# Image keys of ten batches by seven products for eight blocks

## What is computed

```
q = _heads(hidden_states @ to_q_w)                       # (16, 512, 640) @ (640, 640)
h_txt = _sdpa(q, _heads(ehs_txt @ to_k_w), _heads(ehs_txt @ to_v_w))
...
h_ip = _sdpa(q, _heads(ehs_ip @ to_k_ip_w), _heads(ehs_ip @ to_v_ip_w))   # (16, 427, 1024) @ (1024, 640)
out = _merge(h_txt) + _merge(h_obj) + _merge(h_oth) + _merge(h_ip)
out = out @ to_out_w + to_out_b + hidden_states
```

## Time and profile before

| what | us |
|---|---|
| median of 3 runs | 2381.95 (2381.77 to 2382.32) |
| the profiled execution | 2381.67 |
| its span, first to last instruction | 2379.5 |
| TensorE busy | 2365.9 (99%), 12801 matmuls |
| VectorE busy | 1835.2 (77%) |
| ScalarE busy | 1775.6 (75%) |
| GpSimd busy | 412.5 (17%) |

### The profile page before, as it was taken

How to read it: one execution, slowest core, us unless ns; L and a number is a source line. 1 busy time by engine, 2 the same in 40 slices (tenths; PEclk the granted TensorE clock), 3 DMA queues, 4 the chain that set the end, 5 groups by cost and what they waited for, 6 DMA issues and landing times.

```text
span 2379.5 us, 37663 instructions
## 1 busy us (share of the span) xinstructions
PE 2365.9 (99%) x12801; PEld 1805.1 (76%) x12801; DVE 1835.2 (77%) x3291; ACT 1775.6 (75%) x3906; POOL 412.5 (17%) x564
## 2 busy tenths in 40 slices
PE   9999999999999999999999999999999999999999
PEld 8999999998999986566666666666666666666665
DVE  4457777732333489999999999999999999999994
ACT  4343433332223369999999999999999999999995
POOL 0000000000000023413223133133132231231310
PEclk9999999999999999999999999999999999999999
DMA  9445444374644555545555555555455555555542
GB/s 339 161 128 159 150 136 141 109 268 147 232 167 174 182 174 153 148 129 154 152 143 146 134 148 159 137 146 151 128 156 154 134 150 141 144 161 128 147 132 78
DMA packets 371749, 370.12 MB, mean 156 GB/s; under 512 B 110046, under 2 KB 298590, under 8 KB 371558
## 3 DMA queue, kind: packets, MB, share of 16 engines
q1 hardware_dynamic: 334384, 306.14, 46.7%
q10 hardware_dynamic: 37174, 61.59, 7.0%
HBM read 215.57 MB, written 83.89 MB: 126 GB/s over the span
## 4 chain that ended last, share of the span: by engine, by line
PE 97%; ACT 2%; issue 0%; DMA 0%; DVE 0%; ACTq 0%
PE st_ps L1661 17%; PE s_ps L489 13%; PE st_ps L509 12%; PE om_ps L523 12%; PE om_ps L544 11%; PE om_ps L567 11%; PE s_ps L1713 7%; PE om_ps L1713 4%; PE s_ps L1681 3%; PE st_ps L1713 3%; ACT s_ps L689 1%; PE om_ps L1730 1%; ACT probs L681 1%; PE om_ps L602 1%; PE st_ps L1621 0%
## 5 line engine op out<-in xcount | busy, mean ns | idle before, releaser
L689 ACT ACTIVATE s_ps<-s_ps,negmax 128x427 f32<-128x427 f32 x1280 | 767.8, 608 | 21.6 <-DVE small L759 21.6
L750 DVE TENSOR_REDUCE negmax<-s_ps 128x2 f32<-128x854 f32 x640 | 666.0, 1041 | 75.4 <-PE s_ps L489 69.1
L681 ACT ACTIVATE probs<-st_ps 128x1024 f32<-128x1024 f32 x632 | 656.1, 1038 | 15.2 <-PE st_ps L509 3.7
L489 PE MATMUL s_ps<-kpack,qpack 96*128 96x512 f32 x1280 | 420.9, 410 | 2.1 <-ACT s_ps L689 2.1
L509 PE MATMUL st_ps<-qpack,kpack 104*128 104x512 f32 x1264 | 405.4, 402 | 2.5 <-ACT probs L681 2.5
L447 POOL TENSOR_TENSOR small<-small,negmax 128x616 f32<-128x616 f32 x160 | 196.5, 1228 | 999.8 <-DVE negmax L767 999.6
L1661 PE MATMUL st_ps<-ctx_split,w_split_ip 128*128 128x428 f32 x1848 | 364.2, 358 | 0.0
L1661 PEld LDWEIGHTS st_ps<-ctx_split,w_split_ip 128*128 128x128 f32 x1848 | 347.4, 188 | 15.2 <-issue 1.0
L489 PEld LDWEIGHTS s_ps<-kpack,qpack 96*128 96x128 f32 x1280 | 223.4, 189 | 177.6 <-ACT s_ps L689 81.0
L544 PE MATMUL om_ps<-xs,wq 128*128 128x512 f32 x1200 | 340.6, 394 | 0.0
L567 PE MATMUL om_ps<-heads,wo 128*128 128x512 f32 x1125 | 320.8, 394 | 0.0
(11 more groups left out here) (116 smaller groups left out, 2437.8 us busy)
## 6 DMA issues: line engine op xcount, KB each, us to landing
qpack<-q_out SPq DMA_DIRECT2D x240, 256.0 KB, 4.7
kpack<-kT SPq DMA_DIRECT2D x240, 217.5 KB, 2.9
kT<-k_out ACTq DMA_DIRECT2D x154, 217.5 KB, 3.3
ctx_split_raw<-in_ctxT SPq DMA_DIRECT2D x128, 214.0 KB, 4.6
tok_pair<-in_ctxT SPq DMA_DIRECT2D x48, 512.0 KB, 4.7
xs_raw<-in_xT SPq DMA_DIRECT2D x85, 256.0 KB, 3.8
out<-in_xT SPq DMA_DIRECT2D x75, 256.0 KB, 4.0
out_yT<-out SPq DMA_DIRECT2D x75, 256.0 KB, 2.1
```

The lines of the kernel that those rows point to most:

```text
L489: last = nc.tensor.matmul(s_ps[:, n % 2, z, :], qpack[r][0:ROWS_S, j, t * P:(t + 1) * P], kpack[r][0:ROWS_S, j, :], start=True, stop=True)
L681: nc.scalar.activation(probs[:, at:at + 2, :], transposed(u, duo), ACT.Exp).then_inc(p_done, 1)
L689: last = nc.scalar.activation(s_ps[:, n % 2, z, SMALL:TOK], s_ps[:, n % 2, z, SMALL:TOK], ACT.Exp, bias=negmax[:, r, IP, j, t:t + 1], accu ...
L750: nc.vector.tensor_reduce(negmax[:, r, IP, j, t0:t0 + 2], s_ps[:, n % 2, :, SMALL:TOK], AX_X, ALU.max, negate=True).then_inc(s_max, 1)
```

## The change

Batches 1 to 10 are taken in five pairs. The 640 key channels are 4 blocks of 128 and a fifth. For the four, weights are cut in 2 x 2 (512 context channels by 256 key channels) and a pair's context in 2 (halves of the context channels) x 2 (batches), and seven products take the place of eight. The fifth block is computed as before. A pair is 18 groups (`K_GROUPS`: operand, bank, tile) of 12 matmuls. Its eight operands are staged one after the other, as 4 x 428 columns, in three slots (`K_SLOTS`). GpSimd makes the sums T3, T2, T4 and T1 (`key_sum`), VectorE the sums of the weights once (`key_weight_sums`) and ten additions of PSUM banks per pair (`add_group`), two of which leave their sum in SBUF as u3.

Besides: the pairs' stores go to the sync queue (`store_group`), and so do raw loads of 876 KB each (`load_raw`); the small values' steps stand between the first four tiles of text values, and the quarters of the image-value weights are loaded only when the small values are stored; their sums (`weight_sums`) move from tile ("v", 3, 0) to ("v", 0, 0); `wq` and `x` are loaded at the start of batch 11 instead of batch 5.

```diff
+K_OPERANDS = (B11, T3, T2, T4, B21, T1, B22, "B12")
+K_SLOTS = 3
+K_GROUPS = ((0, "X", 0), (0, "X", 1), (0, "F", 0), (1, "Q", 0), (1, "Q", 1), (2, "U", 0), (2, "U", 1),
+            (3, "Q", 0), (3, "Q", 1), (4, "X", 0), (4, "X", 1), (4, "F", 0), (5, "U", 0), (5, "U", 1),
+            (6, "U", 0), (6, "U", 1), (6, "F", 1), (7, "F", 1))
+K_OUT = {7: (0, 2), 8: (0, 3), 9: (0, 0), 10: (0, 1), 11: (0, 4), 12: (1, 2), 13: (1, 3), 14: (1, 0), 15: (1, 1), 17: (1, 4)}
...
     for run in V_TXT:
-        ORDER += [("v", run, t) for t in range(len(tiles(run)))]
+        for t in range(len(tiles(run))):
+            ORDER.append(("v", run, t))
+            if run == V_TXT[0]:
+                ORDER.append(("s", 2 + t, 0))
...
     for run in range(TXT, RUNS):
-        ORDER += [("k", run, m) for m in k_slots(run)]
-        ORDER += {TXT + 1: [("s", 2, 0)], TXT + 2: [("s", 3, 0)]}.get(run, [])
+        if run - TXT not in K_PAIRED:
+            ORDER += [("k", run, m) for m in k_slots(run)]
+        elif K_PAIRED.index(run - TXT) % 2 == 0:
+            ORDER += [("p", K_PAIRED.index(run - TXT) // 2, i) for i in range(len(K_GROUPS))]
...
-    SUMS[("v", 3, 0)] = ("a", 0)
+    SUMS[("v", 0, 0)] = ("a", 0)
...
+    SUMS[("k", before_pairs, 4)] = ("sw", 0)
+    for i, part in ((0, S3), (1, S2), (4, S1), (5, S4)):
+        SPLITS[("p", 0, i)] = [("sw", part, 0)]
+    for pp in range(len(K_PAIRS)):
+        ahead = [("k", before_pairs, 3), ("p", 0, 0)] if pp == 0 else [("p", pp - 1, 15), ("p", pp - 1, 17)]
+        for j, step in enumerate(ahead + [("p", pp, i) for i in (2, 3, 6, 9, 11, 13)]):
+            SPLITS.setdefault(step, []).append(("z", pp, j))
+    T_SUMS = {}
+    for pp in range(len(K_PAIRS)):
+        ahead = [("k", before_pairs, 4), ("p", 0, 0)] if pp == 0 else [("p", pp - 1, 16), ("p", pp, 0)]
+        for i, step in zip((T3, T2, T4, T1), ahead + [("p", pp, 3), ("p", pp, 7)]):
+            T_SUMS[step] = (i, pp)
...
+        def store_group(pp, i):
+            run, m = pair_block(pp, i)
+            k0 = k_num(run, m)
+            sp.wait_ge(k_lo, k0 + 1)
+            sp.wait_ge(k_fill, k0 - k_base(TXT) + 1)
+            for part in (HI, LO):
+                sp.dma_start(d["kT"][run - TXT, part, m * P:(m + 1) * P, N_TXT:TOK],
+                             k_out[:, k0 % KR, part, 0:SM + IPN - 1].bitcast(F32)).then_inc(k_stored[k0 % KR], 16)
...
+        sp.wait_ge(s_acc, 4)
+        sp.wait_ge(sv_stored, 32)
         load_quarter(w_ops_raw[:, LO, A11, :, :], 0, 0)
...
+            elif kind == "z":
...
+                nc.scalar.activation(slots[z % K_SLOTS][:, HI, :, :], z_raw(which, n), ACT.Copy).then_inc(piece_hi, 1)
...
+            elif kind == "z":
...
+                hi, lo, raw = slots[r][:, HI, :, :], slots[r][:, LO, :, :], z_raw(which, n)
...
+        def add_group(pp, i):
...
+            if i in (5, 6):
...
+                nc.vector.tensor_tensor(u2, bank(pp, "U", t), u2, ALU.add).then_inc(u_add, 1)
+                dve.wait_ge(u_add, n + 2 * t + 1)
+                nc.vector.tensor_tensor(u3, bank(pp, "Q", t), u2, ALU.add).then_inc(u_add, 1)
+            elif i in (7, 8, 14, 15):
...
+                nc.vector.tensor_tensor(bank(pp, kind, t), bank(pp, kind, t), u2, ALU.add).then_inc(u_add, 1)
+            elif i in (12, 13):
...
+                nc.vector.tensor_tensor(u3, bank(pp, kind, t), u3, ALU.add).then_inc(u_add, 1)
...
+            if kind == "p":
+                add_group(a, b)
+                if b - 1 in K_OUT:
+                    keep_group(a, b - 1)
+                if b == len(K_GROUPS) - 1:
+                    keep_group(a, b)
...
+        def key_sum(i, pp):
...
+            if i == T3:
...
+                to, a, b, op = t3_raw[:, :, :], b22, b12, ALU.subtract
+            elif i == T2:
...
+                to, a, b, op = t2_raw[:, :, :], t3_raw[:, :, :], b11, ALU.add
+            elif i == T4:
+                stage_done(pool, z_number(pp, 3) - K_SLOTS)
...
+                to, a, b, op = z_raw(pp, 3), b21, t2_raw[:, :, :], ALU.subtract
+            else:
+                stage_done(pool, z_number(pp, 5) - K_SLOTS)
+                to, a, b, op = z_raw(pp, 5), b12, b11, ALU.subtract
+            nc.gpsimd.tensor_tensor(to, a, b, op).then_inc(t_raw, 1)
...
+        def k_group(pp, i):
...
+            if i == 0 or K_GROUPS[i - 1][0] != j:
+                pe.wait_ge(piece_lo, split_upto(("z", pp, j)))
+                if j in (1, 2, 5, 6):
+                    pe.wait_ge(piece_lo, split_upto(("sw", {1: S3, 2: S2, 5: S1, 6: S4}[j], 0)))
...
+            elif i in (7, 8):
+                pe.wait_ge(u_add, U_ADDS * pp + 2 * (t + 1))
```

More of the change, by code:

```diff
@@ L58 @@
 OP_PARTS = ((B11, B22), (B22, T4), (T4, OPS))
+K_PAIRS = ((1, 2), (3, 4), (5, 6), (7, 8), (9, 10))
+K_PAIRED = tuple(b for pair in K_PAIRS for b in pair)
+K_OPERANDS = (B11, T3, T2, T4, B21, T1, B22, "B12")
[4 more added lines that the diff above has]
+K_OUT = {7: (0, 2), 8: (0, 3), 9: (0, 0), 10: (0, 1), 11: (0, 4), 12: (1, 2), 13: (1, 3), 14: (1, 0), 15: (1, 1), 17: (1, 4)}
+K_OUT_ORDER = tuple(K_OUT.values())
+U_ADDS = 10
+S_PARTS = (S1, S2, S3, S4)
 V_TILES = 3
@@ L964, in project_context @@
     assert in_pair1 + pair_size + size(2, 2, CH) <= in_w_ops
+    s_w, s_w_raw = both("s_weights", [P, len(S_PARTS), 2, CC2, 2 * P], in_top)
+    raw = [at(f"ctx_raw{r}", [P, 2, 2, CC2, IPN], F32, at0) for r, at0 in enumerate((in_c0, in_c1))]
+    in_slots = in_top + size(len(S_PARTS), 2, CC2, 2 * P)
+    slot_size = size(2, CC2, IPN)
+    slots, slots_raw = zip(*(both(f"k_ops{r}", [P, 2, CC2, IPN], in_slots + r * slot_size) for r in range(K_SLOTS)))
+    in_sums = in_slots + K_SLOTS * slot_size
+    t3_raw = at("t3_raw", [P, CC2, IPN], F32, in_sums)
+    t2_raw = at("t2_raw", [P, CC2, IPN], F32, in_sums + size(CC2, IPN))
+    u2_k = at("u2_k", [P, 2, IPN], F32, in_sums + 2 * size(CC2, IPN))
+    u3_k = at("u3_k", [P, 2, IPN], F32, in_sums + 2 * size(CC2, IPN) + size(2, IPN))
+    assert in_sums + 2 * size(CC2, IPN) + 2 * size(2, IPN) <= end
     w, w_raw = {"k_txt": w0, "v_txt": w2}, {"k_txt": w0_raw, "v_txt": w2_raw}
@@ L988, in project_context @@
     sv_stored = sem("sv_stored")
+    sq_in, s_sum = sem("sq_in"), sem("s_sum")
+    raw_in = [[[sem(f"raw_in{r}_{h}{k}") for k in range(2)] for h in range(2)] for r in range(2)]
+    t_raw = sem("t_raw")
+    z_acc, u_acc, x_sb, u_add = sem("z_acc"), sem("u_acc"), sem("x_sb"), sem("u_add")
     d["late"] = LateKeys(w_ip, c0, k_late, k_stored, k_fill)
@@ L1006, in landed @@
     def landed(load):
-        return 16 * sum(buffer(n) == buffer(load) for n in range(load + 1))
+        return 16 * sum(buffer(n) == buffer(load) and LOAD_RUN[n] - TXT not in K_PAIRED for n in range(load + 1))
     def is_txt(run):
@@ L1043, in k_base, with k_num @@
         return run * QC
+    def k_num(run, m):
+        b = run - TXT
+        if b not in K_PAIRED:
+            return k_base(run) + m
+        first, second = K_PAIRS[K_PAIRED.index(b) // 2]
+        return k_base(TXT + first) + K_OUT_ORDER.index((b - first, m))
     K_ALL = k_base(RUNS) - DEFER
@@ new lines, in z_raw, with bank @@
+    def z_raw(pp, j):
+        i, (b11, b21, b12, b22) = K_OPERANDS[j], (raw[pp % 2][:, 1 - h, k, :, :] for h in range(2) for k in range(2))
+        in_slot = slots_raw[z_number(pp, j) % K_SLOTS][:, LO, :, :]
+        return {B11: b11, B21: b21, B22: b22, "B12": b12, T3: t3_raw[:, :, :], T2: t2_raw[:, :, :], T4: in_slot, T1: in_slot}[i]
+    def bank(pp, kind, t):
+        if kind == "F":
+            return k_ps[:, (pair_base(pp) + K_OUT_ORDER.index((t, QC - 1))) % 2, 0:IPN]
+        if kind == "U":
+            return t_ps[:, t, 0:IPN]
+        return v_ps[:, "XQ".index(kind), t, 0:IPN]
@@ L1243, in sync_part @@
             load_c(3, n)
+        for h in range(2):
+            sp.wait_ge(s_acc, h + 1)
+            for n in range(CC):
+                load_halves("v", h, n)
+        for n in range(CC):
+            load_c(V_LOAD[0], n)
         sp.wait_ge(t_done, 1)
@@ L1341, in keep_k @@
         def keep_k(run, m):
-            k0, (to, at, n) = k_base(run) + m, k_cols(run)
+            k0, (to, at, n) = k_num(run, m), k_cols(run)
             act.wait_ge(k_acc, k0 + 1)
@@ L1594, in fill_small @@
         def fill_small(run, m):
-            k0, b = k_base(run) + m, run - TXT
+            k0, b = k_num(run, m), run - TXT
             pool.wait_ge(k_hi, k0 + 1)
```

242 lines of the change are left out of this document (217 added, 25 removed).

## The result

| what | before | after |
|---|---|---|
| median of 4 runs, us | 2382.11 | 2401.55 (2401.32 to 2403.3) |
| ratio, 95% interval | | 1.0082 (1.007 to 1.0094) |
| span of the profiled execution, us | 2379.5 | 2399.9 |
| mean granted clock of TensorE | 1.000 | 0.994 |

The change costs 19.4 us, although 120 matmuls are gone. The page of the changed kernel: busy time of the engines, then the chain that ended last, by engine.

A forecast was written before the change was run, and what follows sets the result against it. TensorE bounds the kernel, busy 2365.9 of 2379.5 us. Span 2379.5 - 23.4 + 26.8 + 12.7 + 2.0 + 0.5 = 2398.1; with 2.2 around it and 0.3 to the median, 2400.5 us, range 2380 to 2420.

The forecast's parts named there:

- Matmuls, -23.4: Image keys, batches 1 to 10: 120 fewer matmuls at 0.195 us each, -23.4 us.
- The exclusion: VectorE operations with two SBUF operands and GpSimd sums exclude each other, first come first served, for the whole hold of 3.83 us.
- the rival in which the engines hardly block each other: At the eight long low parts: hardly any blocking, only the first pair stands 1.0 us; 2360 us, chance 0.15.
- GpSimd's sum, 3.83: Each of GpSimd's four sums of 1712 elements per pair takes 3.83 us, at 2.12 ns an element.
- The rival with 3.03: GpSimd's sums run at L447's rate, 3.03 us each, so stands are shorter; 2382.4 us, no change, chance 0.10.
- The layout of a steady pair: TensorE stands before groups 3, 5 and 9: 3.95, 1.1 and 1.7 us, 6.7 a pair, 26.8 for four pairs.
- The clock: After the first pair's long stand TensorE runs at 1.2 GHz for some 4 us, half of it lost: +2.0 us.
- a fall in every pair: Rival: the clock falls in each pair's stand of 4 us, up to 4 x 2.0 us more; 2408 us, chance 0.09.
- The first pair: Weight sums alternate with GpSimd's T3, T2 and T4; TensorE stands 11.0 us, and T1 against B21 adds 1.7.
- The text phase, +0.5: Later weight quarters and sums delay splits for the eighth text-value block: +0.5 us, between 0 and 2.
- Additions into PSUM, 0.6: VectorE adding back into PSUM takes 0.6 us, four per pair, none on the path found.
- Stores, loads, batch 11 at nothing: Stores on the sync queue, raw loads a pair ahead, wq and x loaded at batch 11's start: cost nothing.

The follow-up runs named there:

- the writes: Changed kernel with each of GpSimd's four sums replaced by one constant write, 2360.43 us, or by three, nearly as long as the sum, 2361.71 us.
- the run with that part alone: Kernel before with only the small values' steps moved among the text values, their loads and later weight quarters and sums with them: 2383.19 us, ratio 1.0004.

## Why the prediction was right, and where it was not

The forecast was 2400.5 us and the time is 2401.55. Step by step:

- **Matmuls, -23.4.** Right: 12681 are left, and 24 of them take 4.69 us wherever nothing is late.
- **The exclusion.** Right, and shown by the writes: a hold lasts as long as the sum, for 3.9 us too. No hold was let go early, and the rival in which the engines hardly block each other is out: its 2360 is what the kernels without GpSimd's reads give (2360.43, 2361.71).
- **GpSimd's sum, 3.83.** Measured 3.9 where nothing holds it (3935 and 3955 ns by form), 0.1 over. The rival with 3.03 is out.
- **The layout of a steady pair.** The order was right: T3's low part held by T2, T4 held by that, T2's low part held by T4, B21's by T1. The sizes weren't. T2's sum ended at R+8.7, as laid out (R+8.8), but the held low part only 1.8 behind it, not 1.9 plus a hand-over, and TensorE followed within 0.05, not 0.25. From start to start the stand was 3.54 to 3.58 (forecast 3.95). Before group 9 it was 1.30 to 1.38 (1.7), and the one before group 5, seen when the clock stays up, 0.85 (1.1). Some 5.8 instead of 6.7 a pair: the mis-sized term is the hand-over, 0.25 to 0.4 at each stand.
- **The clock.** Here the forecast failed. It had the clock fall once, behind the first stand, and put a fall in every pair among the rivals with a chance of 0.09. It fell in all of them: 1.4 us in the first pair (2.0 in the sum) and 8.6 in the four steady ones. No row stood behind that chance: the forecast itself says that no row excludes the rival. The rival's own 2408 was too high, since the slow stretch lies over the stand before group 5, which leaves 5.2 us net of its 8, and since the stands were shorter. The Trainium skill, page "TensorE: Matmul & The Clock Gate", part 1, ties the clock to the engine's recent work; the rows 1.00, 0.82 and 0.61 around a stand of 3.4 us agree.
- **So the total was right by two errors that cancel.** Stands and clock were 26.8 + 12.7 + 2.0 = 41.5 in the forecast and 41.3 in the trace, but the four steady pairs have 28.7 of them (26.8) and the first 12.6 (14.7). In a steady pair the stands that are left make 4.9, not 6.7, and 2.2 for the clock weren't in the forecast. That the errors cancel is luck.
- **The first pair.** The stand was 9.76 from start to start (11.0), and the way there was another. The forecast gives times of the kernel before; the key stage begins 11.16 us later in the changed one, so its weight sums at 509 are due at 520.2. They came at 522.63: the sync queue issues the weight quarters at 512.98, behind a wait for the stores of the image values and three raw loads, and VectorE idled 2.30 us for them. A wait on that queue wasn't read. What the error would have cost was kept small by chance: with the quarters late, T3's sum went first and unhindered, and TensorE started at 540.44, where the layout, moved by 11.16, has 541.7. The weight sums were stretched, as forecast, to 2.40, 1.22, 4.99 and 4.69 us for 1.22 each, 13.3 in all where the forecast had 16:

```profile
522.63 2.40 DVE L1715 TENSOR_TENSOR s_weights_raw<-s_weights_raw 128x1024 f32<-128x1024 f32 x1 [2.30 <-DMA s_weights_raw<-in_k_ip]
524.94 1.22 DVE L1716 TENSOR_TENSOR s_weights_raw<-s_weights_raw 128x1024 f32<-128x1024 f32 x1
526.08 4.99 DVE L1718 TENSOR_TENSOR s_weights_raw<-s_weights_raw 128x1024 f32<-128x1024 f32 x1
531.11 4.69 DVE L1720 TENSOR_TENSOR s_weights_raw<-s_weights_raw 128x1024 f32<-128x1024 f32 x1
...
520.00 3.94 POOL L1882 TENSOR_TENSOR t_raw<-ctx_raw 128x1712 f32<-128x1712 f32 x1
```

- **The text phase, +0.5.** No stand at the eighth block: VectorE's sums began at 131.13 (131.7 forecast, and a microsecond more with the later start), and the splits behind them were ready. A price was there elsewhere, in a place that the forecast put at nothing: the image values, 0.9 us. The 0.9 of the run with that part alone is within its interval.
- **Additions into PSUM, 0.6.** Right: 0.61 us (L1740), and on no path.
- **Stores, loads, batch 11 at nothing.** Nothing shows: no idle time of TensorE in the key stage is ended by a DMA or by ScalarE, and batch 11 starts without a stand.
- **Two readings to put right.** The earlier trace rows don't show 8 matmuls that start in 2 us: x8 counts those that the stretch touches, and 8 starts would be 0.25 us apart. The trace has four starting at 6.62 and the next at 7.91, which is the 0.32 us that the forecast uses, so its 1.2 GHz holds. And in the rival with 3.03 us the first pair should read 9.5, not 7.7, by the forecast's own four times 0.8 (12.7 - 3.2), which makes its total 2384. Nothing hangs on it, since the sums take 3.9.

## What to carry to other kernels

Before work is given to GpSimd "because it is idle", list VectorE's operations with two SBUF operands in the same stretch and lay both engines out as one: here VectorE, 7.7 us of work a pair more, was the better place by 28 us, and with the sums placed ahead of need by 35. Count for every stand of a few microseconds also what TensorE's clock takes behind it, and look for what that slow stretch covers. And follow each load of an operand back to the wait in front of it on its queue before giving it a time.

## What the hardware showed beyond that

- A held operation doesn't pay its whole length after the hold: the low parts ended 1.8 us behind the sum that held them (638.78 behind 636.96, 607.00 behind 605.20), where an unhindered one lasts 1.94.
- VectorE's additions with one operand in PSUM aren't held. Beside T1's sum, which runs from 601.31 for 3.89 us, the addition starts and ends as always:

```profile
601.31 3.89 POOL L1882 TENSOR_TENSOR k_ops_raw<-ctx_raw 128x1712 f32<-128x1712 f32 x1 [8.60 <-PE om_ps L1996]
...
601.90 0.60 DVE L1735 TENSOR_TENSOR u_k<-s_ps,u_k 128x428 f32<-128x428 f32 x1
602.42 4.58 DVE L1696 TENSOR_TENSOR k_ops<-ctx_raw,k_ops 128x1712 fp32r<-128x1712 f32 x1
```

- A short operation of GpSimd with one operand is held as well. The fills of 16 columns, 0.20 us alone, took up to 1.76 beside a low part (the mean is 642 ns over the stretch 500 to 790); nobody waited for them here.
- Behind stands of 1.92 us or less TensorE kept its pitch in all these kernels, and behind those of 2.97 us or more it lost 1.4 to 2.9 us; no stand of a length between was seen in the key stages. In the kernel with all sums on VectorE a stand of 2.98 cost 2.9 more, nearly as much as the stand itself.
